# Expert rows added to the output by an accumulating scatter instead of gather, add and scatter

## The chip, the cores and the metric

The kernel runs on one core of a Trainium2 chip. The metric is the device time of one execution in microseconds; the median of the runs shown is compared. Five engines work side by side: TensorE (PE, with its weight loads PEld), VectorE (DVE), ScalarE (ACT), GpSimd (POOL) and SyncE (SP), which here only issues DMAs. They wait for each other and for DMAs through semaphores.

## What is computed

Two layers on 1024 rows (4 x 256) of 256 columns. The first is a selective scan over a context, gated by the normalised rows, and its result is added to the rows. The second, where the change lies, is a mixture of 8 experts with the top 2 chosen per row and room for 320 rows per expert:

```python
xr = x.reshape(S, d)
probs = jax.nn.softmax(xr @ Wg, axis=-1)
gate_vals, expert_idx = jax.lax.top_k(probs, K)
...
kept = pos < C                       # C = 320 slots per expert
...
dispatched = xr[dispatch_mask.reshape(-1) % S].reshape(E, C, d)
h = jax.nn.relu(jnp.einsum('ecd,edf->ecf', dispatched, w1))
expert_out = jnp.einsum('ecf,efd->ecd', h, w2)
...
out = jnp.einsum('ks,ksm->sm', combine_weights, rerouted)
...
x = x + _L0_xattn_ref(ctx_1024, _layernorm(x, axis=-1), ...)
x = x + _L0_ffn_ref(_layernorm(x, axis=-1), ...)
```

So each output row is its row after the first layer plus, for each of its two experts that had room, the gate times the expert's result.

## The kernel before

The scan layer runs first, in two halves of 512 rows; VectorE's scans set its pace. Then rows are routed: each row's two copies, 256 columns with the gate and the row's own number behind them (258 in all), are scattered by GpSimd into a table in HBM, `expert_rows`, of 8 x 320 slots (`send`, L309). This table was filled early by SyncE from one constant row, `fill` (L214), in which the gate is 0 and the row number 8192, beyond the last row. So a slot that no row took carries a number that later DMAs skip. SyncE also stores the rows after the first layer, `x1`, to `out` (L233).

Then come the 8 experts, one after the other. For each of them SyncE loads the slots' rows `xe` and the weights `w1raw` and `w2raw`, 1024 KB each. Every product is done in three matmuls, of a rounded part (`...hi`) and the rest (`...lo`) of each operand, in chunks of 320 columns. ScalarE makes the `hi` parts. VectorE makes `w1lo`, `xtlo` and `htlo`, and GpSimd makes `w2lo` in four pieces per expert (`low_w2`, L345), the last two of which only VectorE makes for expert 7. TensorE runs the first product (`xthi`, `w1hi`, 8 chunks, L864 to L866), the second (`hthi`, `w2hi`, 8 chunks, six matmuls each, the same lines), and the turning of the rows (L873) and of the results (L882). The results of expert e - 1 are turned after the second chunk of expert e's first product. For experts 0 to 6 TensorE, ScalarE and VectorE loop; GpSimd's and SyncE's streams are written out.

The results go to `out` as follows. GpSimd gathers, with three indirect DMAs per expert (128, 128 and 64 rows), the 320 output rows so far into `so_far` (`fetch`, L350; L358). It may do so only when the scatters of the expert before have landed (`res_out`). VectorE multiplies a turned result by the gate, adds `so_far` and writes `eo` (`gated_rows`, L1256; L1263), between its fourth and fifth `htlo` of the next expert. GpSimd scatters `eo` to `out` with three indirect DMAs (`send_results`, L362; L367), between the second and third piece of `w2lo` of the next expert. For the last expert all this stands at the end of the program.

A DMA on GpSimd's queue (q0) is built by GpSimd itself, which is busy for it (`DMA_INDIRECT` rows); SyncE's (q1) are not.

Of the kernel before, what the change touches and what calls it, by code (L numbers as in the profile page):

```python
# [28 lines left out]
P = 128  # L29
# [18 lines left out]
DROPPED = 8192.0  # L48
EPS = 1e-5
# [5 lines left out]
NCONST = CIOTA + NE  # L55
# [19 lines left out]
def build(nc, x, ctx_t, inproj_t, xproj_t, dtproj_t, conv_w, chan, wg, w1, w2, consts, slot_numbers, sel,  # L75
# [3 lines left out]
    with ExitStack() as ctx:  # L79
# [56 lines left out]
        def sm(name, shape, dt=F32):  # L136
# [43 lines left out]
        so_far = sb("so_far", [P, ET, DM])  # L180
# [16 lines left out]
            "h_psum hthi_done htlo_done o_psum o_done r_psum so_far_set so_far_in0 so_far_in1 so_far_in2 r_done res_out x1_out dve_step").split()}  # L197
# [5 lines left out]
        def _(sp):  # L203
            sp.dma_start(inps, inproj_t).then_inc(s["inp_in"], 16)
            for hb in range(HALVES):
# [7 lines left out]
            sp.wait_ge(s["fill_made"], 1)  # L213
            sp.dma_start(xe_dram.rearrange("(t p) r -> p t r", p=P),  # L214
                         fill[:, None, :].to_broadcast([P, SLOTS // P, ROW])).then_inc(s["xe_filled"], 16)

# [46 lines left out]
        def _(pool):  # L263
# [3 lines left out]
            nc.gpsimd.memset(fill[:, 0:DM + 1], 0.0)  # L267
            nc.gpsimd.memset(fill[:, DM + 1:ROW], DROPPED).then_inc(s["fill_made"], 1)

# [68 lines left out]
            pool.wait_ge(s["xe_filled"], 16)  # L338
# [12 lines left out]
            def fetch(e):  # L351

                pool.wait_ge(s["meta_done"], 2 * (e + 1))
                if e >= 1:

                    pool.wait_ge(s["res_out"], 16 * ET * e)
                for t in range(ET):
                    nc.gpsimd.indirect_dma_start(  # L358
                        so_far[0:EROWS[t], t, :], None, out,
                        bass.IndirectOffsetOnAxis(ap=dst[0:EROWS[t], e * ET + t, :], axis=0),  # L360
                        bounds_check=T - 1, oob_is_err=False).then_inc(s[f"so_far_in{t}"], 16)

            def send_results(e):

                for t in range(ET):
                    pool.wait_ge(s["r_done"], ET * e + t + 1)
                    nc.gpsimd.indirect_dma_start(  # L367
                        out, bass.IndirectOffsetOnAxis(ap=dst[0:EROWS[t], e * ET + t, :], axis=0),
                        eo[0:EROWS[t], t, :], None, bounds_check=T - 1, oob_is_err=False
                    ).then_inc(s["res_out"], 16)  # L370


            pool.wait_ge(s["xthi_done"], KC)
            nc.gpsimd.memset(so_far[:], 0.0).then_inc(s["so_far_set"], 1)
            pool.wait_ge(s["so_far_set"], 1)
            pool.wait_ge(s["x1_out"], 16 * HALVES)
            for e in range(NE):
                pool.wait_ge(s["w2_in"], 16 * (e + 1))

                for m in range(WP // 2 if e == NE - 1 else WP):  # L380
                    low_w2(e, m)
                    if m == WP // 2 - 1 and e >= 1:
                        send_results(e - 1)
                fetch(e)
            send_results(NE - 1)


# [584 lines left out]
        def _(dve):  # L972
# [283 lines left out]
            def gated_rows(e):  # L1256

                dve.wait_ge(s["r_psum"], e + 1)
                for t in range(ET):

                    dve.wait_ge(s[f"so_far_in{t}"], 16 * (e + 1))
                    rows = slice(0, EROWS[t])
                    nc.vector.scalar_tensor_tensor(  # L1263
                        out=eo[rows, t, :], in0=ps[rows, 6 + t // 2, (t % 2) * DM:(t % 2 + 1) * DM],
                        scalar=gates[rows, bass.ds(e * ET + t, 1), 0], in1=so_far[rows, t, :],
                        op0=ALU.mult, op1=ALU.add).then_inc(s["r_done"], 1)
# [36 lines left out]
            expert(0, True, False)  # L1303
            with dve.Fori(1, NE - 1) as e:
                expert(e, False, False)
            expert(NE - 1, False, True)
# [54 lines left out]
```

## Time and profile before

| | us |
|---|---|
| three runs | 354.39, 355.7, 356.2; median 355.7 |
| profiled execution, span | 353.9 |
| TensorE busy | 276.9 (78%) |
| VectorE busy | 266.8 (75%) |
| GpSimd busy | 234.3 (66%) |
| ScalarE busy | 170.6 (48%) |
| GpSimd: 24 gathers into `so_far` | 28.4 |
| GpSimd: 24 scatters to `out` | 23.7 |

The page of the profile has a span only, from the first to the last instruction; the time of a run is measured around it. The rows further down are of five views. The table by stage gives each engine's busy time in a stretch of the span. The chain of waits follows the work that ended last back to the start. The timeline shows single instructions of an engine, with the idle time before each in brackets and what ended it. The groups by line give counts and means, and the DMA view the queues and issues. Matmuls overlap in the pipeline: a row of TensorE shows 0.31 us, but the next one starts 0.15 us later.

### The profile page before, as it was taken

The page shows a single profiled execution, that of the slowest core. Times are in us where ns is not written, and L with a number is a line of the kernel's source. Part 1 is how long each engine was busy: PE and PEld are TensorE (multiplying, and loading weights), DVE is VectorE, ACT ScalarE, POOL GpSimd, SP SyncE. Part 2 cuts the span into 40 slices and gives each one's busy share as a digit, 9 for nine tenths or more (in the row PEclk, how much of TensorE's full clock was granted, in tenths as well). Part 3 has the DMA queues.
Part 4 walks back from the last instruction along what each step waited for, and adds up shares of the span by engine and source line. Part 5 has one row for each costly group of instructions (what it writes and reads, how often), then busy time and mean ns, then how long its engine had stood idle before and what let it go on. Part 6 is the DMA issues. An engine that isn't in the chain of part 4 may idle for free.

```text
span 353.9 us, 5109 instructions
## 1 busy us (share of the span) xinstructions
PE 276.9 (78%) x1684; PEld 242.0 (68%) x1684; DVE 266.8 (75%) x373; ACT 170.6 (48%) x308; POOL 234.3 (66%) x144
## 2 busy tenths in 40 slices
PE   7889187746456588666669698889999999999970
PEld 6334175635346377555569688889999999999970
DVE  1489999999999999999997664167566675857610
ACT  0498366654825423327741236084647474554600
POOL 0125999987799948443548248738686777768643
PEclk9969679896959986988888879999999999999995
DMA  7940000000030000000005502654645545454210
GB/s 253 303 115 3 0 0 1 2 0 0 0 119 3 0 0 2 0 1 2 1 15 210 189 23 100 217 179 172 245 161 190 184 148 183 159 216 174 89 49 33
DMA packets 13504, 33.10 MB, mean 94 GB/s; under 512 B 2602, under 2 KB 9268, under 8 KB 11216
## 3 DMA queue, kind: packets, MB, share of 16 engines
q1 hardware_dynamic: 10240, 25.92, 21.7%
q0 software_dynamic: 2816, 6.32, 5.1%
q10 hardware_dynamic: 432, 0.65, 0.7%
q8 instruction: 9, 0.15, 0.2%
q14 instruction: 7, 0.06, 0.0%
HBM read 25.50 MB, written 8.43 MB: 96 GB/s over the span
## 4 chain that ended last, share of the span: by engine, by line
PE 33%; DVE 31%; issue 15%; DMA 8%; POOL 5%; ACT 4%; SPq 1%; POOLq 0%; DVEq 0%
DVE h L1061 16%; PE ps L864 9%; PE ps L866 8%; PE ps L865 8%; DVE hc L1072 4%; POOL expert_rows L316 4%; DMA xnat<-in_x 2%; PE ps L680 2%; DMA w1raw<-in_w 2%; PE ps L873 2%; DMA expert_rows<-xrow,sloti 2%; PE ps L882 1%; DVE dbu L1180 1%; DVE delta L1026 1%; PE ps L851 1%
## 5 line engine op out<-in xcount | busy, mean ns | idle before, releaser
L293 POOL TENSOR_TENSOR dbu<-du,bsb 128x1024 f32<-128x1024 f32 x30 | 101.1, 3392 | 29.0 <-DVE h L1061 23.1
L1061 DVE TENSOR_TENSOR_SCAN h<-da,dbu 128x1024 f32<-128x1024 f32 x32 | 100.6, 3144 | 0.1
L680 PEld LDWEIGHTS ps<-cst,hc 128*128 128x128 f32 x512 | 74.7, 225 | 5.5 <-issue 2.2
L680 PE MATMUL ps<-cst,hc 128*128 128x128 f32 x512 | 74.6, 309 | 0.0
L673 PE MATMUL ps<-stack,sels 96*128 96x512 bf16 x32 | 14.4, 451 | 55.3 <-DVE hc L1072 55.3
L1252 DVE SCALAR_TENSOR_TENSOR htlo<-ps,hthi 128x320 fp32r<-128x320 f32 x64 | 30.4, 486 | 34.1 <-ACT hthi L588 34.0
L462 ACT ACTIVATE bsb<-ps 128x512 f32<-128x512 f32 x32 | 18.8, 593 | 63.1 <-PE ps L667 61.9
L348 POOL TENSOR_TENSOR w2lo<-w2raw,w2hi 128x512 fp32r<-128x512 f32 x30 | 38.2, 1300 | 12.8 <-ACT w2hi L579 12.6
L673 PEld LDWEIGHTS ps<-stack,sels 96*128 96x128 bf16 x32 | 3.2, 101 | 63.0 <-DVE hc L1072 54.1
L480 ACT ACTIVATE da<-delta,anegs 128x510 f32<-128x510 f32 x64 | 41.9, 712 | 0.0
L864 PE MATMUL ps<-xthi,w1hi 128*128 (+1 forms) x128 | 40.6, 317 | 1.0 <-DVE w1lo L1169 1.0
L864 PE MATMUL ps<-hthi,w2hi 128*128 128x320 f32 x128 | 40.4, 315 | 1.3 <-issue 1.3
L866 PE MATMUL ps<-xthi,w1lo 128*128 (+1 forms) x128 | 39.7, 310 | 0.0
L865 PE MATMUL ps<-xtlo,w1hi 128*128 (+1 forms) x128 | 39.6, 310 | 0.0
L866 PE MATMUL ps<-hthi,w2lo 128*128 128x320 f32 x128 | 39.6, 309 | 0.0
L865 PE MATMUL ps<-htlo,w2hi 128*128 128x320 f32 x128 | 39.5, 309 | 0.0
L1072 DVE TENSOR_TENSOR hc<-h,ps 128x1024 f32<-128x1024 f32 x32 | 38.1, 1191 | 0.3 <-PE ps L680 0.3
L588 ACT ACTIVATE hthi<-ps 128x320 fp32r<-128x320 f32 x64 | 27.6, 436 | 14.8 <-PE ps L866 14.8
L316 POOL DMA_INDIRECT expert_rows<-xrow,sloti x16 | 22.0, 1377 | 19.2 <-issue 10.3
L367 POOL DMA_INDIRECT out<-eo,dst x24 | 23.7, 986 | 16.5 <-DVE eo L1263 11.9
L358 POOL DMA_INDIRECT so_far<-out,dst x24 | 28.4, 1182 | 8.7 <-issue 6.0
L1169 DVE TENSOR_TENSOR w1lo<-w1raw,w1hi 128x512 fp32r<-128x512 f32 x32 | 31.9, 1055 | 2.1 <-ACT w1hi L518 2.1
(142 smaller groups left out, 483.2 us busy)
## 6 DMA issues: line engine op xcount, KB each, us to landing
w1raw<-in_w SPq DMA_DIRECT2D x8, 1024.0 KB
w2raw<-in_w SPq DMA_DIRECT2D x8, 1024.0 KB, 4.8
expert_rows<-fill SPq DMA_DIRECT2D x1, 2580.0 KB, 17.8
xe<-expert_rows SPq DMA_DIRECT2D x8, 258.0 KB, 5.7
xnat<-in_x SPq DMA_DIRECT2D x1, 1024.0 KB, 8.7
out<-x SPq DMA_DIRECT2D x2, 512.0 KB, 4.1
sels<-in_sel SPq DMA_DIRECT2D x1, 768.0 KB, 9.9
xe<-expert_rows SPq DMA_DIRECT2D x8, 64.5 KB, 5.5
```

Source lines behind the costliest of these rows:

```text
L293: nc.gpsimd.tensor_tensor(dbu[r][:], du[:, :, halves(hb)], bsb[r][:, None, :].to_broadcast([P, EC, HT]), ALU.mult).then_inc(s["dbu_done"], 1)
L316: nc.gpsimd.indirect_dma_start(xe_dram, bass.IndirectOffsetOnAxis(ap=sloti[:, j, k:k + 1], axis=0), xrow[:, j, k, :], None, bounds_check=S ...
L348: nc.gpsimd.tensor_tensor(w2lo[:, fs, :], w2raw[:, fs, :], w2hi[:, fs, :].bitcast(F32), ALU.subtract).then_inc(s["w2lo_done"], 1)
L480: nc.scalar.activation(da[g % RING][:, c, :].rearrange("p (b l) -> p b l", b=HB)[:, :, 1:L], delta[:, c, halves(hb)].rearrange("p (b l) -> ...
L680: ins = nc.tensor.matmul(y[:, t, c * P:(c + 1) * P], hc[par][:, c, t * P:(t + 1) * P], ident, start=False, stop=last, skip_group_check=True)
L864: nc.tensor.matmul(out_, hi_a, hi_b, start=start, stop=False)
L865: nc.tensor.matmul(out_, hi_a, lo_b, start=False, stop=False)
L866: return nc.tensor.matmul(out_, lo_a, hi_b, start=False, stop=stop)
L1061: nc.vector.tensor_tensor_scan(h[r][:].rearrange("p c t -> p (c t)"), da[r][:].rearrange("p c t -> p (c t)"), dbu[r][:].rearrange("p c t - ...
L1072: nc.vector.tensor_tensor(hc[r % SUMS][:], h[r][:], ps[:, bank:bank + 1, :].to_broadcast([P, EC, HT]), ALU.mult).then_inc(s["mult_done"], 1)
L1169: nc.vector.tensor_tensor(w1lo[:, :, cols], w1raw[:, :, cols], w1hi[:, :, cols].bitcast(F32), ALU.subtract).then_inc(s["w1lo_done"], 1)
L1252: nc.vector.scalar_tensor_tensor(out=htlo[:, f, :], in0=ps[:, f % 4, 0:CAP], scalar=0.0, in1=hthi[:, f, :].bitcast(F32), op0=ALU.max, op1= ...
```

## The change

The gather `fetch`, its buffer `so_far`, the memset of it and four semaphores are gone. VectorE's `gated_rows` multiplies by the gate alone, with a `tensor_scalar`, and waits before that until all scatters of the expert before have landed. The scatters to `out` (`add_results`) now add to the rows in HBM (`compute_op=ALU.add`). `out` has 320 more rows, which the host cuts off. An empty slot carries the number of one of them in place of 8192: `fill` is all zeros, and a second DMA on SyncE writes a constant column of spare row numbers into the table once the fill has landed. The fill itself now waits for the constants to be loaded. VectorE's expert loop is written out.

```diff
+SPARE = CAP
+FROWS = SLOTS // P
...
+CSPARE = CIOTA + NE
+NCONST = CSPARE + 2 * FROWS
...
             sp.wait_ge(s["fill_made"], 1)
+            sp.wait_ge(s["small_in"], 64)
             sp.dma_start(xe_dram.rearrange("(t p) r -> p t r", p=P),
                          fill[:, None, :].to_broadcast([P, SLOTS // P, ROW])).then_inc(s["xe_filled"], 16)
+
+            sp.wait_ge(s["xe_filled"], 16)
+            sp.dma_start(xe_dram.rearrange("(t p) r -> p t r", p=P)[:, :, DM:ROW],
+                         cst[:, CSPARE:CSPARE + 2 * FROWS].rearrange("p (t o) -> p t o", o=2)
+                         ).then_inc(s["xe_filled"], 16)
...
-            nc.gpsimd.memset(fill[:, 0:DM + 1], 0.0)
-            nc.gpsimd.memset(fill[:, DM + 1:ROW], DROPPED).then_inc(s["fill_made"], 1)
+            nc.gpsimd.memset(fill[:], 0.0).then_inc(s["fill_made"], 1)
...
-            pool.wait_ge(s["xe_filled"], 16)
+            pool.wait_ge(s["xe_filled"], 32)
...
-            def fetch(e):
-
-                pool.wait_ge(s["meta_done"], 2 * (e + 1))
-                if e >= 1:
-
+            def add_results(e):
+
+                if e:
                     pool.wait_ge(s["res_out"], 16 * ET * e)
-                for t in range(ET):
-                    nc.gpsimd.indirect_dma_start(
-                        so_far[0:EROWS[t], t, :], None, out,
-                        bass.IndirectOffsetOnAxis(ap=dst[0:EROWS[t], e * ET + t, :], axis=0),
-                        bounds_check=T - 1, oob_is_err=False).then_inc(s[f"so_far_in{t}"], 16)
-
-            def send_results(e):
-
                 for t in range(ET):
                     pool.wait_ge(s["r_done"], ET * e + t + 1)
                     nc.gpsimd.indirect_dma_start(
                         out, bass.IndirectOffsetOnAxis(ap=dst[0:EROWS[t], e * ET + t, :], axis=0),
-                        eo[0:EROWS[t], t, :], None, bounds_check=T - 1, oob_is_err=False
+                        eo[0:EROWS[t], t, :], None, bounds_check=T + SPARE - 1, compute_op=ALU.add
                     ).then_inc(s["res_out"], 16)
 
 
-            pool.wait_ge(s["xthi_done"], KC)
-            nc.gpsimd.memset(so_far[:], 0.0).then_inc(s["so_far_set"], 1)
-            pool.wait_ge(s["so_far_set"], 1)
             pool.wait_ge(s["x1_out"], 16 * HALVES)
...
                     if m == WP // 2 - 1 and e >= 1:
-                        send_results(e - 1)
-                fetch(e)
-            send_results(NE - 1)
+                        add_results(e - 1)
+            add_results(NE - 1)
...
                 dve.wait_ge(s["r_psum"], e + 1)
+                if e:
+                    dve.wait_ge(s["res_out"], 16 * ET * e)
                 for t in range(ET):
-
-                    dve.wait_ge(s[f"so_far_in{t}"], 16 * (e + 1))
                     rows = slice(0, EROWS[t])
-                    nc.vector.scalar_tensor_tensor(
-                        out=eo[rows, t, :], in0=ps[rows, 6 + t // 2, (t % 2) * DM:(t % 2 + 1) * DM],
-                        scalar=gates[rows, bass.ds(e * ET + t, 1), 0], in1=so_far[rows, t, :],
-                        op0=ALU.mult, op1=ALU.add).then_inc(s["r_done"], 1)
+                    nc.vector.tensor_scalar(
+                        eo[rows, t, :], ps[rows, 6 + t // 2, (t % 2) * DM:(t % 2 + 1) * DM],
+                        gates[rows, e * ET + t, :], None, ALU.mult).then_inc(s["r_done"], 1)
...
-            expert(0, True, False)
-            with dve.Fori(1, NE - 1) as e:
-                expert(e, False, False)
-            expert(NE - 1, False, True)
+            for e in range(NE):
+                expert(e, e == 0, e == NE - 1)
             gated_rows(NE - 1)
...
+    consts[:, CSPARE + 1:CSPARE + 2 * FROWS:2] = T + np.arange(SLOTS).reshape(FROWS, P).T % CAP
...
-    out = nc.dram_tensor("out", [T, DM], F32, kind="ExternalOutput").ap()
+    out = nc.dram_tensor("out", [T + SPARE, DM], F32, kind="ExternalOutput").ap()
```

On GpSimd, from the scatters of expert 5's results to the end of the program (before):

```order
L367 DMA out<-eo,dst 1024x256 [waits r_done] x3
L348 TENSOR_TENSOR w2lo<-w2raw,w2hi 128x512 [waits w2hi_done] x2
L358 DMA so_far<-out,dst 128x256 [waits res_out,meta_done]
L358 DMA so_far<-out,dst 128x256
L358 DMA so_far<-out,dst 64x256
L348 TENSOR_TENSOR w2lo<-w2raw,w2hi 128x512 [waits w2hi_done,w2_in]
L348 TENSOR_TENSOR w2lo<-w2raw,w2hi 128x512 [waits w2hi_done]
L367 DMA out<-eo,dst 1024x256 [waits r_done] x3
L358 DMA so_far<-out,dst 128x256 [waits res_out,meta_done]
L358 DMA so_far<-out,dst 128x256
L358 DMA so_far<-out,dst 64x256
L367 DMA out<-eo,dst 1024x256 [waits r_done] x3
```

The same stretch after:

```order
L364 DMA out<-eo,dst 1344x256 [waits r_done,res_out]
L364 DMA out<-eo,dst 1344x256 [waits r_done] x2
L355 TENSOR_TENSOR w2lo<-w2raw,w2hi 128x512 [waits w2hi_done] x2
L355 TENSOR_TENSOR w2lo<-w2raw,w2hi 128x512 [waits w2hi_done,w2_in]
L355 TENSOR_TENSOR w2lo<-w2raw,w2hi 128x512 [waits w2hi_done]
L364 DMA out<-eo,dst 1344x256 [waits r_done,res_out]
L364 DMA out<-eo,dst 1344x256 [waits r_done] x2
L364 DMA out<-eo,dst 1344x256 [waits r_done,res_out]
L364 DMA out<-eo,dst 1344x256 [waits r_done] x2
```

The gathers with their wait for `res_out` are gone, the wait stands at the first scatter, and the third and fourth piece of `w2lo` still stand behind the three scatters.

On VectorE, the last expert's chunks to the end (before; `htlo` is the rest of a chunk of the first product, `eo` the gated results):

```order
L1252 SCALAR_TENSOR_TENSOR htlo<-ps,hthi 128x320 [waits hthi_done] x4
L1263 SCALAR_TENSOR_TENSOR eo<-ps,gates,so_far 128x256 [waits so_far_in0,r_psum]
L1263 SCALAR_TENSOR_TENSOR eo<-ps,gates,so_far 128x256 [waits so_far_in1]
L1263 SCALAR_TENSOR_TENSOR eo<-ps,gates,so_far 64x256 [waits so_far_in2]
L1252 SCALAR_TENSOR_TENSOR htlo<-ps,hthi 128x320 [waits hthi_done] x2
```

The same rows after:

```order
L1245 SCALAR_TENSOR_TENSOR htlo<-ps,hthi 128x320 [waits hthi_done] x4
L1256 TENSOR_SCALAR eo<-ps,gates 128x256 [waits res_out,r_psum]
L1256 TENSOR_SCALAR eo<-ps,gates 128x256
L1256 TENSOR_SCALAR eo<-ps,gates 64x256
L1245 SCALAR_TENSOR_TENSOR htlo<-ps,hthi 128x320 [waits hthi_done] x2
```

Nothing moved: the three waits for gathered rows became one, for the scatters of the expert before.

## Rows read from the trace of the kernel before

**Rows 1.** Table by stage: stretch, length, busy (instructions) per engine, clock, DMA share, GB/s.
```profile
224.00:240.70 16.70, 15.10 (x100) 13.63 (x98) 8.78 (x24) 8.91 (x18) 8.66 (x8) 1.00 0.70 249
...
304.50:320.40 15.90, 15.90 (x109) 15.41 (x109) 10.35 (x22) 8.91 (x18) 11.77 (x11) 1.00 0.52 184
...
336.40:354.00 17.60, 6.85 (x47) 6.31 (x45) 1.83 (x4) 0.88 (x2) 6.87 (x7) 0.74 0.13 42
```

**Rows 2.** Chain of waits at the end: start, length, what.
```profile
336.70 2.76 DMA out<-eo,dst
...
343.01 2.39 DMA so_far<-out,dst
```

**Rows 3.** Timeline of TensorE: start, length, line, operation, tiles, [idle before <- releaser].
```profile
320.34 0.41 PE L864 MATMUL ps<-hthi,w2hi 128*128 128x320 f32 x1
...
323.96 0.31 PE L864 MATMUL ps<-hthi,w2hi 128*128 128x320 f32 x1
...
342.91 0.55 PE L882 MATMUL ps<-cst,eot 128*128 128x128 f32 x3 [0.20 <-ACT eot L602]
```

**Rows 4.** Timeline of VectorE: `eo` of expert 6, then of expert 7.
```profile
332.74 1.25 DVE L1263 SCALAR_TENSOR_TENSOR eo<-ps,gates,so_far 128x256 f32<-128x256 f32 x3
...
343.49 0.48 DVE L1263 SCALAR_TENSOR_TENSOR eo<-ps,gates,so_far 128x256 f32<-128x256 f32 x1 [6.71 <-PE ps L882]
...
345.42 0.48 DVE L1263 SCALAR_TENSOR_TENSOR eo<-ps,gates,so_far 64x256 f32<-64x256 f32 x1 [0.38 <-DMA so_far<-out,dst]
```

**Rows 5.** Timeline of GpSimd: last scatter of expert 5, then those of expert 7.
```profile
320.77 0.92 POOL L367 DMA_INDIRECT out<-eo,dst  x1 [0.30 <-issue]
...
344.81 1.04 POOL L367 DMA_INDIRECT out<-eo,dst  x1 [0.86 <-DVE eo L1263]
346.15 1.00 POOL L367 DMA_INDIRECT out<-eo,dst  x1 [0.31 <-DVE eo L1263]
347.45 0.92 POOL L367 DMA_INDIRECT out<-eo,dst  x1 [0.30 <-issue]
```

**Rows 6.** Timeline of GpSimd: `w2lo` and gathers in a steady expert, and the first gather.
```profile
321.70 2.57 POOL L348 TENSOR_TENSOR w2lo<-w2raw,w2hi 128x512 fp32r<-128x512 f32 x2
...
326.06 1.46 POOL L358 DMA_INDIRECT so_far<-out,dst  x1 [0.30 <-issue]
...
329.78 1.29 POOL L348 TENSOR_TENSOR w2lo<-w2raw,w2hi 128x512 fp32r<-128x512 f32 x1 [1.02 <-ACT w2hi L579]
...
225.32 1.06 POOL L358 DMA_INDIRECT so_far<-out,dst  x1 [0.15 <-issue]
```

**Rows 7.** Timeline of TensorE: its waits in the first expert.
```profile
225.90 1.21 PE L873 MATMUL ps<-cst,xe 128*128 128x128 f32 x6 [0.63 <-DMA xe<-expert_rows]
...
231.79 0.41 PE L864 MATMUL ps<-xthi,w1hi 128*128 x1 [0.97 <-DVE w1lo L1169]
```

**Rows 8.** Chain of waits, first expert.
```profile
223.67 6.46 DMA w1raw<-in_w
```

**Rows 9.** Timeline of SyncE: the load of expert 0's first weights.
```profile
96.91 0.34 SPq L218 DMA_DIRECT2D w1raw<-in_w  x1
```

**Rows 10.** Table by stage, as rows 1, where that load has ended.
```profile
101.50:102.50 1.00, 1.00 (x4) 0.69 (x3) 1.00 (x1) 0.11 (x1) 0.99 (x1) 0.50 0.00 0
```

**Rows 11.** DMA queues from 225 to 230.12: packets, MB, share of 16 engines.
```profile
q1 hardware_dynamic: 257, 1.62, 91.5%
q0 software_dynamic: 2, 0.01, 0.4%
```

**Rows 12.** Groups by line of VectorE: count, busy us, mean ns, idle before.
```profile
L1045 DVE TENSOR_SCALAR spr<-ps,ch 128x512 f32<-128x512 f32 x2 | 1.5, 751 | 0.2 <-ACT hc L424 0.2
```

**Rows 13.** Table by stage, as rows 1, after expert 5's scatters.
```profile
322.50:323.00 0.50, 0.50 (x6) 0.50 (x5) 0.50 (x1) 0.50 (x2) 0.50 (x2) 1.00 0.00 0
```

**Rows 14.** DMA issues: count, KB each, us to landing.
```profile
expert_rows<-fill SPq DMA_DIRECT2D x1, 2580.0 KB, 17.8
```

**Rows 15.** DMA queues from 333 to 340, as rows 11.
```profile
q0 software_dynamic: 128, 0.26, 10.5%
```

More of the change, by code:

```diff
@@ L54 @@
 CIOTA = CDST + TILES
-NCONST = CIOTA + NE
+CSPARE = CIOTA + NE
+NCONST = CSPARE + 2 * FROWS
 BC = 2 * DS
@@ L179, in build @@
         eo = sb("eo", [P, ET, DM])
-        so_far = sb("so_far", [P, ET, DM])
         ps = ctx.enter_context(nc.psum_tensor("ps", [P, 8, HT], F32))
@@ L196, in build @@
             "w1hi_done w1lo_done w2hi_done w2lo_done xet_psum xthi_done xtlo_done meta_done "
-            "h_psum hthi_done htlo_done o_psum o_done r_psum so_far_set so_far_in0 so_far_in1 so_far_in2 r_done res_out x1_out dve_step").split()}
+            "h_psum hthi_done htlo_done o_psum o_done r_psum r_done res_out x1_out dve_step").split()}
         block = ctx.enter_context(nc.Block())
@@ L1356 @@
         ins[name] = nc.dram_tensor("in_" + name, a.shape, mybir.dt.from_np(a.dtype), kind="ExternalInput").ap()
-    out = nc.dram_tensor("out", [T, DM], F32, kind="ExternalOutput").ap()
+    out = nc.dram_tensor("out", [T + SPARE, DM], F32, kind="ExternalOutput").ap()
     build(nc, out=out, **ins)
     r = run_bass_kernel_spmd(nc, [feed], core_ids=[0])
-    return r.results[0]["out"].reshape(B, L, DM)
+    return r.results[0]["out"][0:T].reshape(B, L, DM)
```

## Prediction

> **What bounds the kernel now.** I read the busy shares first, then the table by stage, then the chain of waits, and last the timelines of the three places where the edited instructions sit. No engine fills the whole span, so the shares say little by themselves. The stages say more: in a steady expert TensorE is busy for the whole stretch, 15.90 of 15.90 us at a granted clock of 1.00 (the 2.4 GHz level), while GpSimd, which issues the gathers and scatters that change, is busy for 11.77 [rows 1]. There a microsecond taken off GpSimd is worth nothing, and one added costs nothing until TensorE has to wait for something that GpSimd makes. TensorE is idle in two places of the expert stage: at the first expert (busy 15.10 of 16.70 us) and at the end (6.85 of 17.60) [rows 1]. So the change can gain in these two places alone, and it can lose in all of them.
>
> The chain of waits looks as if the end held a gain. It goes from expert 6's last scatter (336.70, landing after 2.76) to the gather of expert 7's rows (the last one issued at 343.01, landing after 2.39) and on to the third `eo` [rows 2]: some 6 us, from 339.46 to 345.40, with the gather on the chain. The timeline tells another story. TensorE finishes the last transposes at 342.91 + 0.55 = 343.46 [rows 3], and VectorE's first `eo` starts at 343.49, after 6.71 us of waiting for TensorE [rows 4]: its gathered rows were already there. It ends at 343.97; GpSimd's first scatter follows 0.84 us later, at 344.81, and from there the three scatters run at GpSimd's own pace, 344.81, 346.15, 347.45, with 0.31 and 0.30 us between them [rows 5]. The third `eo` did wait 0.38 us for gathered rows, but it ended at 345.42 + 0.48 = 345.90 [rows 4]; with the same 0.84 its scatter could have gone at 346.74, and it went at 347.45. The chain follows the wait that ended last on VectorE; the pace of the scatters hides that wait.
>
> **The change part by part.** *The 24 gathers go, with `so_far`'s memset.* In the steady experts they stand between the last `w2lo` (end 321.70 + 2.57 = 324.27) and the next expert's first (329.78), which waits 1.02 us more for ScalarE's `w2hi` [rows 6]: nothing is gained, GpSimd only waits longer for the same ScalarE. At the end they run beside TensorE's last matmuls, as just shown: without them the first `eo` still starts at 343.49 and its scatter at 344.81. Gain there: 0. The memset stands ahead of expert 0's `w2lo`; TensorE would begin expert 0's second product that much sooner, and would then wait longer at 225.90 for expert 1's rows, which it does already for 0.63 us [rows 7]. Gain: 0.
>
> *The gathers' traffic goes.* TensorE's wait at 231.79 (0.97 us, for `w1lo` [rows 7]) goes back to the load of expert 1's `w1raw`, 6.46 us from its issue at 223.67 [rows 8]. The same 1024 KB for expert 0, issued at 96.91 with nothing beside them, were moved by 101.50: no byte after that [rows 9, 10]. Expert 0's gathers are issued from 225.32 on [rows 6], in the middle of the slow load; taking them out could give back up to the 0.97 us. But between 225 and 230.12 the gathers' queue moved 2 packets, 0.01 MB, against 1.62 MB on the loads' queue [rows 11]: they waited for the load, the load did not wait for them. I take 0, and keep 0.97 as the most that could be won.
>
> *VectorE multiplies by the gate and no longer adds.* One `eo` took 0.48 us for 256 columns [rows 4]. The nearest row for the new form, a `tensor_scalar` out of PSUM, is 0.751 for 512 [rows 12], so the new one lies between half of that and all of it: -0.10 to +0.27 for the first `eo` (the others are behind the pace of the scatters). It is nearest to today's 0.48, if a fixed part is allowed for; I take 0. The expert loop on VectorE is written out instead of looped; VectorE was busy 10.35 of 15.90 us [rows 1], so this costs nothing as long as the instructions arrive.
>
> *A new wait on VectorE.* Ahead of the three `eo` it now waits until the scatters of the expert before have landed, since `eo` is what they read and no gather stands between any more. Queued behind it are the later `htlo`, on which TensorE waits. In the steady state an expert's last scatter is issued at 320.77, and the DMA engines are quiet from 322.50 on [rows 5, 13]; the next `eo` comes at 332.74 [rows 4]. That is 10 us of cover. At the end it is 343.49 against 336.70 + 2.76 = 339.46, 4.0 us [rows 2, 4]. I cost it at 0.
>
> *On SyncE the fill of the slot rows* now waits for the small loads, and a second DMA writes each slot's spare row number, 2560 pieces of 8 bytes. The fill is as many pieces of 1032 bytes and took 17.8 us [rows 14]. Twice that, one after the other, ends some 40 us into the span; SyncE's next work waits until 96.91 [rows 9], and the first scatter into these rows comes far later still. 0.
>
> *The scatter accumulates.* This is where the cost is, and no row of this kernel shows such an operation. It has two prices.
>
> First its issue on GpSimd. A plain scatter takes 1.04, 1.00 and, with half the rows, 0.92 us [rows 5]: nearly all of it is fixed, and 64 rows fewer save about 0.1. An accumulating one must name the old row, the source row and the row written, three addresses in place of two; at half again of the part that grows with the rows that is 0.1 + 0.1 + 0.05 = **0.25 us** per expert. Bounds: 0 below, since nothing is left out; above, the dearest indirect DMA of the steady experts, a gather at 1.46 [rows 6], hence 3 x 1.46 - 2.96 = 1.42. I take 0.25, nearest to how the plain rows behave.
>
> What an expert can bear follows from the same timeline. GpSimd's third `w2lo` follows the scatters; one takes 1.29, so it is done at 321.70 + 1.29 = 322.99 [rows 6]. TensorE's second product starts at 320.34 and meets that `w2lo` at its fifth chunk, 323.96 [rows 3]. The slack is **0.97 us** per expert. 0.25 fits, so the steady experts stay TensorE's: 0. At the end there is no cover: **+0.25**.
>
> Second its landing, which only the last scatter shows. A plain one lands 2.76 us after its issue begins; the gather's trip is 2.39 [rows 2], less 0.92 of issue [rows 5] 1.47. If the old row were fetched, and only then the whole of the plain scatter followed, that trip would come on top. Bounds: 0 (the same bytes are still written) and 1.47. Part of that trip is the completion, which isn't paid twice, so I take **+0.8**.
>
> A scatter also writes all 320 slots now, the empty ones to spare rows; the bytes are few: three scatters moved 0.26 MB in 10.5% of 7 us, 0.74 us of all engines [rows 15]. The Trainium skill ("Collectives: The Full Stack", section "The bandwidth ceiling: the fold count and why AG ≠ RS ≠ AR") speaks against the change here: it finds that adding in the DMA path halves the rate, not through the arithmetic but because two sources are read. No run yet shows that for this queue; by it alone the last scatter's fifth of those 0.74 us would double, +0.15 in place of 0.8, and the sum would be +0.4.
>
> Sum: 0 + 0 + 0.25 + 0.8 = **+1.05 us** on the profiled execution, from a span of 353.9 to about 355.0. The median of the three runs, 355.7, lies 1.8 above that span; the same difference gives **356.7**.
>
> **The rivals.** *A. The issue outgrows its cover.* From 0.97 us per expert on, the third `w2lo` is late for TensorE, and each of the experts 1 to 6 pays the rest, shifting all that follows. For: nothing shows that an accumulating scatter is built the way of a plain one, and GpSimd alone builds it. Against: the plain rows hardly grow with their count. At the bound of 1.42 it is 6 x 0.45 = 2.7, plus 1.42 and 0.8 at the end: +4.9, 360.6. At twice the plain price (+2.96) it is 6 x 1.99 = 11.9, plus 2.96 and 0.8: +15.7, 371.
>
> *B. The cover holds, the landing is long.* 128 rows over 16 DMA engines are 8 each; if their reads and writes don't overlap, the landing grows by several trips of 1.47. Two make +2.9 + 0.25: 358.9. Eight would make 11.8, and then the wait on VectorE binds too (4.0 us of cover at the end).
>
> *C. The gather was on the path after all,* as the chain of waits says: up to the 6 us from 339.46 to 345.40 would go, 350. Against: the first `eo` started 0.03 us after TensorE. What remains possible is the 0.97 us at 231.79, which is under the measure of "no change".
>
> **How the numbers follow.** A measurement of this kernel can tell about 0.5%, 1.8 us, from no change. The forecast with its bounds (0 to +1.7, and less when the load of `w1raw` gains) has 0.53; A near its bound (+2 to +5.3) 0.21, A far above it 0.12; B from 1.8 up 0.09; C and all other gains over 1.8 us 0.05. Faster 0.05, same 0.53, slower 0.42. The range: at the low end the forecast with 0.97 won and little paid, 354.9; at the high end A's bound, 361.0. Outside lie A far above, the longest part of B, and C. The likeliest case's own range is 354.9 to 357.5.
>
> **What would show it.** In the profile after: steady experts of 15.9 us again with TensorE full, and no wait of the `hthi,w2hi` matmuls for GpSimd's `w2lo`; the first scatter of expert 7 about 1.35 us after TensorE's last transpose ends; scatters of 1.0 to 1.2 us; the end of the span about a microsecond further from the last issue. Scatters above 1.3 us and waits of TensorE for `w2lo` make it A; several us more between the last issue and the end make it B; a first scatter sooner than 1.3 us after the last transpose makes it C. The forecast is wrong if TensorE's stretch per expert grows at all.

## The result, and the profile after

The changed kernel is slower: 362.67 us, median of 4 runs (361.75 to 363.37), against 355.54 (354.39 to 356.2, 4 runs) for the kernel before. The ratio is 1.0191 (95% interval 1.0166 to 1.0216). The profiled execution has a span of 360.2 us, 6.3 more than before. The prediction said 356.7 and at most 361.0; it was wrong.

The timeline of GpSimd in the changed kernel, one steady expert and then the end (start, length, line, operation, tiles, [idle before <- releaser]):

```profile
289.13 1.56 POOL L364 DMA_INDIRECT out<-eo,dst  x1 [1.07 <-DVE eo L1256]
290.99 1.55 POOL L364 DMA_INDIRECT out<-eo,dst  x1 [0.30 <-issue]
292.84 1.43 POOL L364 DMA_INDIRECT out<-eo,dst  x1 [0.30 <-issue]
...
351.45 1.55 POOL L364 DMA_INDIRECT out<-eo,dst  x1 [5.12 <-DVE eo L1256]
353.30 1.55 POOL L364 DMA_INDIRECT out<-eo,dst  x1 [0.30 <-issue]
355.16 1.43 POOL L364 DMA_INDIRECT out<-eo,dst  x1 [0.30 <-issue]
```

They answer to [rows 5]: 1.55, 1.55 and 1.43 us in place of 1.04, 1.00 and 0.92. Three issues cost 4.53 us, 1.57 more than before. (Two of the 24 took 1.87 and 1.93 us; the mean of all is 1.56.) That is over the 0.97 us that an expert could bear, so TensorE waits. Its waits from 224 us on (engine, line, waited for: us in total, times, longest):

```profile
PE ps L857 <- POOL w2lo L355: 6.2, 6, 1.4
PE ps L866 <- DMA xe<-expert_rows: 1.1, 1, 1.1
```

The first row did not exist before. By stretch (length, then busy time and count for PE, PEld, DVE, ACT, POOL, then clock, DMA share, GB/s), 100 us of steady experts of the kernel before and, under it, of the changed one:

```profile
240.00:340.00 100.00, 100.00 (x679) 97.26 (x680) 63.80 (x123) 54.11 (x110) 72.52 (x62) 1.00 0.47 167
```

```profile
240.00:340.00 100.00, 93.80 (x630) 89.81 (x629) 65.29 (x111) 51.04 (x105) 56.36 (x41) 1.00 0.56 152
```

GpSimd is busy for 16 us less in this stretch and delays TensorE nevertheless, because of where its work stands. The chain of waits of the changed kernel through one expert (start, length, what) goes round in a loop that TensorE is hardly part of:

```profile
287.80 1.26 DVE eo L1256 x3
...
289.13 0.36 POOL out L364
...
290.99 1.55 POOL out L364
...
292.84 1.43 POOL out L364
294.27 2.56 POOL w2lo L355 x2
296.90 5.12 DMA w2raw<-in_w
...
304.25 0.45 ACT hthi L581
...
305.13 1.26 DVE eo L1256 x3
```

Scatters, the last two `w2lo`, then the reload of the one `w2raw` buffer that these two free, then ScalarE's work on it, then the next `eo` and its scatters: 17.33 us for this turn, where an expert of TensorE's work is 15.9.

The timeline of VectorE gives the rest: the first `eo` of expert 0, of expert 6 and of expert 7.

```profile
236.06 1.25 DVE L1256 TENSOR_SCALAR eo<-ps,gates 128x256 f32<-128x256 f32 x3
...
339.53 1.25 DVE L1256 TENSOR_SCALAR eo<-ps,gates 128x256 f32<-128x256 f32 x3
...
350.12 1.26 DVE L1256 TENSOR_SCALAR eo<-ps,gates 128x256 f32<-128x256 f32 x3 [6.54 <-PE ps L875]
```

In the kernel before, expert 0's stood at

```profile
237.14 1.25 DVE L1263 SCALAR_TENSOR_TENSOR eo<-ps,gates,so_far 128x256 f32<-128x256 f32 x3
```

and the other two at 332.74 and 343.49 [rows 4]. Behind the last landing SyncE waits for the program's end; I call this the close. First the kernel before, then the changed one (queue, line, waited for: us, times, longest):

```profile
SPq L79 <- PEq L79: 4.0, 1, 4.0
```

```profile
SPq L82 <- PEq L82: 1.6, 1, 1.6
```

So the 6.3 us are made up thus (the last issues end at 348.37 and 356.59):

| stretch | before | after | difference |
|---|---|---|---|
| start to first `eo` of expert 0 | 237.14 | 236.06 | -1.08 |
| six experts | 95.60 | 103.47 | +7.87 |
| expert 6's to expert 7's first `eo` | 10.75 | 10.59 | -0.16 |
| to the end of the last issue | 4.88 | 6.47 | +1.59 |
| to its landing, and from there to the end | 5.5 | 3.6 | -1.9 |

### The profile page after: what moved, and what is told of

It is laid out like the page before. It is cut to its first block, busy times and chain, and to the rows that moved or that the text cites. A ratio compares the mean times of both kernels' runs of the same rounds, so it can differ in the third digit from the quotient of the medians.

```text
span 360.2 us, 4914 instructions
## 1 busy us (share of the span) xinstructions
PE 278.0 (77%) x1684; PEld 242.1 (67%) x1684; DVE 272.8 (76%) x373; ACT 169.6 (47%) x308; POOL 218.9 (61%) x118
## 3 DMA queue, kind: packets, MB, share of 16 engines
q0 software_dynamic: 3712, 4.74, 8.5%
## 4 chain that ended last, share of the span: by engine, by line
DVE 32%; issue 19%; PE 14%; POOL 13%; DMA 12%; ACT 6%; SPq 1%; POOLq 1%; DVEq 0%; ACTq 0%
DVE h L1054 16%; DMA w2raw<-in_w 7%; POOL out L364 6%; DVE hc L1065 5%; POOL w2lo L355 4%; PE ps L857 3%; POOL expert_rows L323 2%; PE ps L859 2%; PE ps L858 2%; DMA xnat<-in_x 2%; DVE eo L1256 2%; PE ps L673 2%; ACT hthi L581 2%; DMA xe<-expert_rows 2%; DMA expert_rows<-xrow,sloti 1%
## 5 line engine op out<-in xcount | busy, mean ns | idle before, releaser
L355 POOL TENSOR_TENSOR w2lo<-w2raw,w2hi 128x512 fp32r<-128x512 f32 x30 | 40.9, 1485 | 43.1 <-ACT w2hi L572 43.1
L364 POOL DMA_INDIRECT out<-eo,dst x24 | 37.5, 1561 | 18.4 <-DVE eo L1256 13.5
L1162 DVE TENSOR_TENSOR w1lo<-w1raw,w1hi 128x512 fp32r<-128x512 f32 x32 | 37.7, 1237 | 3.2 <-ACT w1hi L511 3.2
L581 ACT ACTIVATE hthi<-ps 128x320 fp32r<-128x320 f32 x64 | 27.7, 436 | 13.3 <-PE ps L859 13.2
L857 PEld LDWEIGHTS ps<-hthi,w2hi 128*128 128x128 f32 x128 | 24.0, 188 | 9.3 <-issue 8.8
```

The lines of the kernel that those rows point to most:

```text
L355: nc.gpsimd.tensor_tensor(w2lo[:, fs, :], w2raw[:, fs, :], w2hi[:, fs, :].bitcast(F32), ALU.subtract).then_inc(s["w2lo_done"], 1)
L364: nc.gpsimd.indirect_dma_start(out, bass.IndirectOffsetOnAxis(ap=dst[0:EROWS[t], e * ET + t, :], axis=0), eo[0:EROWS[t], t, :], None, boun ...
L581: nc.scalar.activation(hthi[:, f, :], ps[:, f % 4, 0:CAP], ACT.Relu).then_inc(s["hthi_done"], 1)
L857: nc.tensor.matmul(out_, hi_a, hi_b, start=start, stop=False)
L1162: nc.vector.tensor_tensor(w1lo[:, :, cols], w1raw[:, :, cols], w1hi[:, :, cols].bitcast(F32), ALU.subtract).then_inc(s["w1lo_done"], 1)
```

## The experiments

Where a run has one execution, times below are of that one. Seventeen runs of the kernel before lie between 354.49 and 357.58 us, so steps of some tenths are read from the trace, between `eo` and `eo`, and not from such a time.

### The scatter without the add

```diff
-                        eo[0:EROWS[t], t, :], None, bounds_check=T + SPARE - 1, compute_op=ALU.add
+                        eo[0:EROWS[t], t, :], None, bounds_check=T + SPARE - 1
```

> The changed kernel with the addition taken out of the scatter: the same 24 scatters with the same spare rows overwrite instead of adding, so the second expert's result replaces the first one's. Theory (the issue of an accumulating scatter on GpSimd outgrew its cover): the scatters fall from 1.56, 1.55, 1.43 us back to about 1.04, 1.00, 0.92; the distance from one expert's first eo to the next falls from 17.2 us to 15.9; the wait of TensorE for w2lo (6.2 us in all) goes; span about 352.5. Rival (the longer issue comes from the spare rows, every slot being written, or from the bounds check that no longer skips): the scatters stay near 1.5 us and the span near 360. Rival (VectorE's written-out loop costs the time): the scatters fall, the span stays above 358.

Measured: 354.92 us, span 352.9. First the group of the scatters in the changed kernel, then in this one (line, operation, tiles, count | busy us, mean ns of one | idle before):

```profile
L364 POOL DMA_INDIRECT out<-eo,dst x24 | 37.5, 1561 | 18.4 <-DVE eo L1256 13.5 <-issue 4.9
```

```profile
L364 POOL DMA_INDIRECT out<-eo,dst x24 | 23.1, 965 | 23.4 <-DVE eo L1256 18.5 <-issue 4.9
```

The six experts are back at 15.93 us each (238.13 to 333.73), and TensorE does not wait for `w2lo`. One argument of one call carries the whole loss; spare rows, the new DMA and the written-out loop carry none of it. Both kernels write all 320 slots, so the 0.6 us an issue (1561 against 965 ns) are the price of the add alone.

### One, then two of the three scatters add

```diff
-                        eo[0:EROWS[t], t, :], None, bounds_check=T + SPARE - 1, compute_op=ALU.add
+                        eo[0:EROWS[t], t, :], None, bounds_check=T + SPARE - 1, **(dict(compute_op=ALU.add) if t in (0,) else {})
```

> The changed kernel with only the first of each expert's three scatters adding, the other two overwriting (the sums of the rows of slots 128 to 319 are left out). By the rows of before an expert bears 0.97 us more on GpSimd. Theory: the issue grows by 0.55 us, under that, and the experts stay at 15.9 us from eo to eo; span about 352.7. Rival (any lengthening costs, since the loop through w2raw has no slack): about a third of the loss, 16.4 us per expert, span about 355.

Measured: 356.62 us, span 354.5; six experts from 238.41 to 334.66, 16.04 each, and no wait of TensorE for GpSimd. 0.56 us of extra issue cost 0.11. There is a cover, as the theory said. (The span is nearer to the rival's 355, but that is the start: expert 0's `eo` came at 238.41, where the changed kernel had it at 236.06.)

With `t in (0, 1)`:

> As the run with one, but the first two of three scatters add (the sums of slots 256 to 319 are left out). Theory: the issue grows by 1.1 us, 0.13 above the cover of 0.97: 16.0 to 16.2 us from eo to eo, span 353.5 to 354.5. Rival (any lengthening costs): two thirds of the loss, 16.8 us per expert, span about 357.5.

Measured: 360.55 us, span 358.4; 238.17 to 338.20, 16.67 each. TensorE's waits:

```profile
PE ps L857 <- POOL w2lo L355: 2.8, 6, 1.0
```

About 1.1 us of extra issue cost 0.74, and the third add (1.6 in all) brings it to 1.31. The theory's 16.0 to 16.2 was missed; the rival's 16.8 is nearer. The loss begins earlier than at 0.97 and then grows by a little more than the issue grows, which suggests that something beside the third `w2lo` waits for GpSimd.

### A second buffer for w2raw

```diff
+        w2raws = [w2raw, sb("w2odd", [P, FC, DM])]
...
-                sp.wait_ge(s["w2lo_done"], WP * e)
-                sp.dma_start(w2raw[:], w2[e]).then_inc(s["w2_in"], 16)
+                sp.wait_ge(s["w2lo_done"], WP * e - 1)
+                sp.dma_start(w2raws[e % 2][:], w2[e]).then_inc(s["w2_in"], 16)
```

(and the readers of the buffer take it by the expert's parity)

> The changed kernel with a second buffer for w2raw, so that the next expert's second weights are requested when three of the four w2lo pieces are done and not behind the last. The scatters, their place and the rest stay. Theory (two things wait on GpSimd's longer issue: TensorE for the third w2lo piece, at issue minus cover, 1.58 - 0.97 = 0.6 us an expert, and the reload of the one w2raw buffer, which closes a loop scatter, w2lo, reload, w2hi, eo, scatter, and adds the other 0.7): without the second the first eo of each expert lies 16.4 to 16.6 us after the one before instead of 17.24, ScalarE's waits for w2raw (4.3 us in the changed kernel) are gone, TensorE's for w2lo stay (3 us and more), and the whole is 358 to 359 us. Rival (the excess over 0.6 comes from the w2lo pieces that run slower beside w1lo, 3.0 for 2.57 us, or from the adds' traffic): 17.1 to 17.3 us an expert and 361.5 to 363.5 us.

Measured: 362.33 us, span 360.0; 237.79 to 339.25, 16.91 each. ScalarE's waits for `w2raw` are gone, and the expert is 0.33 us shorter than the changed kernel's 17.24. The theory wanted 16.4 to 16.6 us an expert and 358 to 359 us in all, the rival 17.1 to 17.3 and 361.5 to 363.5: the experts lie between the two, the time in the rival's range. (The span is hardly shorter than the changed kernel's, 360.0 against 360.2, since expert 0's `eo` came 1.73 us later here.) So the loop of the chain above is not the price by itself: with it opened, an expert still takes 16.91. The rows say why. TensorE's waits, then a steady stretch of exactly one expert of this kernel, and under it one of the kernel before:

```profile
PE ps L859 <- POOL w2lo L356: 4.4, 6, 0.8
```

```profile
288.52:305.43 16.91, 16.19 (x110) 15.45 (x109) 11.49 (x21) 8.84 (x19) 9.63 (x7) 1.00 0.57 163
```

```profile
284.94:300.88 15.94, 15.94 (x110) 15.46 (x109) 10.38 (x22) 8.91 (x20) 11.80 (x10) 1.00 0.54 184
```

And TensorE around its stop, ahead of the fifth chunk of the second product:

```profile
295.52 0.31 PE L861 MATMUL ps<-hthi,w2lo 128*128 128x320 f32 x1
296.55 0.41 PE L859 MATMUL ps<-hthi,w2hi 128*128 128x320 f32 x1 [0.72 <-POOL w2lo L356]
296.80 0.30 PE L860 MATMUL ps<-htlo,w2hi 128*128 128x320 f32 x1
```

TensorE waits 0.73 us an expert (4.4 / 6), against 0.6 worked out, and its busy time is 16.19 where as many matmuls took 15.94 without a stop: the stop costs 0.25 us beyond the wait. The rows show where: matmuls that follow each other start 0.15 us apart, but the last one before the stop is counted for its whole 0.31, and after the first one behind the stop the next starts only 0.25 later. That is 0.16 + 0.10. And 15.94 + 0.25 + 0.73 = 16.92. (The rival's slower `w2lo` is not there: the timeline's 3.0 us for the two begin before the last scatter's row has ended, and in the chain above they take 2.56 from its end.) So of the changed kernel's 1.31 us per expert, about 0.98 are the late third `w2lo`, and up to 0.33 the late reload. The smaller share is rough: in the changed kernel's one trace the experts vary from 17.08 to 17.56 us, and with VectorE's loop rolled again (below) they take 17.05, which would leave 0.14 for the reload.

### The scatters behind all w2lo pieces

```diff
-                    if m == WP // 2 - 1 and e >= 1:
-                        add_results(e - 1)
+                if e >= 1:
+                    add_results(e - 1)
```

> The changed kernel with one move: the three accumulating scatters of expert e-1 stand behind all pieces of w2lo of expert e on GpSimd, not between the second and the third. Theory: what cost the time is only that the third and fourth w2lo stand behind a dearer issue, and with them the next load of w2raw. The scatters stay at 1.5 us each, but nothing that TensorE waits for is behind them: 15.9 us from eo to eo, no wait for w2lo, span about 352.4, time about 354.8, 0.2% under the kernel before. Rival (the accumulating transfers, longer on the DMA engines, hold back the weight loads): from eo to eo stays above 16.5 us and the span above 356.

Measured: 354.8 us (12 runs) against 355.92 (17 runs), ratio 0.9975 (0.9956 to 0.9995). The scatters are no cheaper:

```profile
L364 POOL DMA_INDIRECT out<-eo,dst x24 | 39.3, 1637 | 13.0 <-DVE eo L1256 7.1 <-issue 5.8
```

but nothing that TensorE soon waits for stands behind them. In the timeline of GpSimd all four `w2lo` run together and the adds follow:

```profile
283.15 5.05 POOL L355 TENSOR_TENSOR w2lo<-w2raw,w2hi 128x512 fp32r<-128x512 f32 x4 [5.07 <-ACT w2hi L572]
288.36 1.56 POOL L364 DMA_INDIRECT out<-eo,dst  x1 [0.16 <-issue]
290.23 1.55 POOL L364 DMA_INDIRECT out<-eo,dst  x1 [0.30 <-issue]
```

Six experts take 238.42 to 334.03, 15.93 each, as the theory said. The same adds, the same bytes on the same queue, cost the six experts nothing: the loss was the dearer issue at its place in GpSimd's order, not the traffic of the adds. This version beats both kernels, the one before by a quarter of a per cent, which is just clear of the noise. Its trace does not show that gain: the execution traced was the slowest of the twelve (357.05 us, span 354.9).

The same move in the kernel before:

> The kernel before with an expert's plain scatters behind all the w2lo pieces of the next, gathers and all else as they were; asks how much of the late run's time is the order alone. Theory (before, TensorE waits for nothing that the order changes: the steady stage is full of TensorE work at 15.90 us): same within 0.5 us, 355.0 to 356.2 us, eo 15.9 us apart. Rival (the gathers now follow the scatters' landing later, so that the sum of scatter, landing, gather and its landing does not fit in an expert any more): eo 16.1 us apart or more and 357 us or more.

Measured: 360.23 us (4 runs), ratio 1.0127 (1.0093 to 1.0161), and 16.61 us an expert (238.10 to 337.77): the rival. VectorE's timeline has the reason, in the worst expert:

```profile
301.94 0.99 DVE L1263 SCALAR_TENSOR_TENSOR eo<-ps,gates,so_far 128x256 f32<-128x256 f32 x2
306.18 0.48 DVE L1263 SCALAR_TENSOR_TENSOR eo<-ps,gates,so_far 64x256 f32<-64x256 f32 x1 [3.25 <-DMA so_far<-out,dst]
```

The gather may only follow the landing of the scatters, and its rows came too late; TensorE then waited 2.4 us for `eo`. So the late order is open only to the kernel without the gather: that is what the change is worth.

### VectorE's loop rolled again

```diff
-            for e in range(NE):
-                expert(e, e == 0, e == NE - 1)
+            expert(0, True, False)
+            with dve.Fori(1, NE - 1) as e:
+                expert(e, False, False)
+            expert(NE - 1, False, True)
```

> The changed kernel with VectorE's expert loop rolled again, as it was before. Theory (the unrolled loop costs and gives nothing): first eo of each expert 17.1 to 17.4 us apart, 361.5 to 363.5 us. Rival (a part of the excess over issue minus cover is VectorE fetching unrolled code): 16.5 to 16.9 us apart and 357 to 360.5 us.

Measured: 362.81 us, span 360.8; 237.80 to 340.12, 17.05 each, 0.05 under the range of the theory and 0.15 over the rival's, with the time in the theory's. The written-out loop is not the cause; the run without the add had it too and took 15.93. Whether it has a part in the last 0.19 us per expert, one execution does not tell.

### The kernel before without its gathers

```diff
-                fetch(e)
+                pool.wait_ge(s["meta_done"], 2 * (e + 1))
```

(and `eo` without `so_far`, as in the changed kernel)

> The kernel before with its gathers taken out and nothing else moved: plain scatters that skip rows numbered above the output, VectorE's loop as it was, and the rows of each expert overwrite instead of being summed. What is left out: the sum over experts. Question: the kernel before ends 4.07 us after its last scatter has landed, the changed one 1.67 us. Theory (GpSimd's closing work grows with the gathers that it issued): 1.5 to 2.1 us from the last landing to GpSimd's end, time 353 to 354.5 us. Rival (it comes from the skipping of rows, or from the rolled loop): about 4.0 us, time 354.8 to 356.2 us. On the head: with no gathers beside it, w1raw of expert 1 takes 5.3 to 6.0 us from its request to the first w1hi piece, 6.48 before.

Measured: 353.61 us, span 351.7. SyncE's wait at the end:

```profile
SPq L79 <- PEq L79: 2.1, 1, 2.1
```

2.1 against 4.0, with rows still skipped and the loop still rolled, as the theory said: the long close belongs to the gathers. (Whether to gathers as such or to the number of indirect DMAs, 48 against 24 in the expert stage, was not told apart.) By the two traces this is nearly all that the gathers cost the kernel before: the spans differ by 2.2 us, the close by 1.9, and the six experts take 95.60 in both. It lies where no row of the prediction was looking. On the head `w1raw` took 5.12 us, a little under the theory's range.

### The last expert alone gathers

```diff
+            pool.wait_ge(s["res_out"], 16 * ET * (NE - 1))
+            for t in range(ET):
+                nc.gpsimd.indirect_dma_start(
+                    so_far[0:EROWS[t], t, :], None, out,
...
+            add_results(NE - 1)
```

(on top of the late order; the last expert's scatters are plain)

> The changed kernel with the adds of an expert behind all its w2lo pieces (as in the run with them late), and the last expert alone done in the old way: its rows so far are gathered once the adds of expert 6 have landed, VectorE adds them, and its three scatters are plain. The spare rows of the output are set to zero once, early. If the last expert's accumulating issues and their longer landing are what its end costs (3 x 0.55 to 0.6 on the issues, 0.5 on the landing, against the plain form), and three gathers do not bring back the long close (4.07 us in the kernel before, 1.67 after), 2.0 us come off the late run: 352.3 to 353.3 us. Rival 1 (any gather brings the long close, or the gathers land too late for VectorE, which wants them at 343 us): 354.3 to 356 us. Rival 2 (the close grows with the number of gathers, 24 before and 3 here): between, 352.8 to 353.6 us.

Measured: 355.51 us (12 runs), ratio to the kernel before 0.9997 (0.9975 to 1.0019): no gain over the late order. The close stays short, 2.2 us, so rival 2 and the first half of rival 1 fall, but the gathers land too late, the second half of rival 1. VectorE:

```profile
345.70 0.48 DVE L1270 SCALAR_TENSOR_TENSOR eo<-ps,gates,so_far 128x256 f32<-128x256 f32 x1 [8.29 <-DMA so_far<-out,dst]
```

That `eo` comes 12.34 us after expert 6's in place of 10.75. The 1.6 us lost are about the 1.5 that the cheaper issues give back.

### Expert 0's gathers made small

```diff
-                        so_far[0:EROWS[t], t, :], None, out,
+                        so_far[0:16 if e == 0 else EROWS[t], t, :], None, out,
```

> The kernel before with expert 0's three gathers cut to 16 rows each, and nothing else; what is left out: most rows that expert 0 would add to. Theory (in the first expert the load of w1raw runs beside the gathers and is slowed by them): from its request to the first w1hi piece 5.4 to 5.9 us, 6.48 before, and TensorE's wait of 0.97 for w1lo there is gone or under 0.3 us; the time is 354.3 to 355.3 us. Rival (the gathers do nothing to the load, and the changed kernel's earlier w1raw comes from something else): 6.3 to 6.6 us, a wait of 0.8 to 1.1 us, 355.0 to 356.2 us.

Measured: 354.83 us, span 353.0. The first `w1hi` of expert 1 on ScalarE, in this kernel and then in the changed one:

```profile
229.26 2.19 ACT L518 ACTIVATE w1hi<-w1raw 128x512 fp32r<-128x512 f32 x4 [1.94 <-DMA w1raw<-in_w]
```

```profile
229.10 2.19 ACT L511 ACTIVATE w1hi<-w1raw 128x512 fp32r<-128x512 f32 x4 [1.39 <-DMA w1raw<-in_w]
```

From the request of `w1raw` (223.30 here, 223.50 there) this is 5.96 and 5.60 us, against 6.48 before: just over the theory's range, and under the rival's. TensorE's wait for `w1lo` shrank to 0.58 from 0.97, less than the theory said. Over all runs: 6.48 and 6.24 in the two kernels with all of expert 0's gathers, 5.12 to 5.92 in eight without any, but 6.47 in the run with the second buffer, which has none either. So the gathers seem to slow this load, by 0.3 to 1.4 us, and something else can too.

Whether that is time is another matter, since TensorE's clock differs there between the runs. The table by stretch has, in the run without the add,

```profile
228.00:230.00 2.00, 2.00 (x10) 2.00 (x10) 0.82 (x1) 0.53 (x1) 0.00 (x0) 0.58 1.06 426
```

a granted clock of 0.58, near the 1.2 GHz level, where the kernels before and after kept 1.00 (the 2.4 GHz level). The same stretch shows 0.50 to 0.60 in six runs, all without gathers beside that load; in all six TensorE had waited 1.1 to 1.9 us for expert 1's rows (`xe`) before. But it had waited 1.35 and 1.49 us in two runs that kept 1.00, so what makes the clock fall is not shown. From the request of `w1raw` to expert 0's first `eo` it takes 13.47 and 13.20 us with all gathers, 12.08 to 12.92 with none or small ones where the clock stayed at 1.00, and 13.46 to 13.77 without gathers where it fell. Expert 0's first `eo` thus lies anywhere from 236.06 to 238.42 in the runs with no gather beside that load, and the -1.08 of the table above is one draw of that; it can't be counted as a gain.

## Why the prediction was wrong, step by step

*The issue of the accumulating scatter* is the step that failed. It was taken at +0.25 us an expert, with 1.42 as the upper bound; it is +1.57. The reasoning was that the price of a plain issue is nearly all fixed, so that a third address could only add to the part that grows with the rows. The add is a fixed price too: 0.51 us for 64 rows and for 128 about as much (1.43 for 0.92, 1.55 for 1.04 and 1.00). The bound was no bound either, since it came from a plain operation; nothing in the trace was an add. And 0.97 lay between the value taken and that bound, so the whole verdict hung on a term that no row showed. The signs that the prediction named for rival A, scatters above 1.3 us and TensorE waiting for `w2lo`, are both there.

*The cover of 0.97 us* was read correctly for the wait that it is of, TensorE for the third `w2lo`: with one add the cover nearly held (0.11 us lost), and with the reload out of the way, 1.57 - 0.97 = 0.60 showed as a wait of 0.73. But rival A's formula (each expert pays the rest) left out two things. A TensorE that stops loses 0.25 us beyond the wait. And the pieces behind the scatters free `w2raw`, whose reload was already late in the kernel before, as ScalarE's waits in its steady stage show, a row that the prediction did not use. It stands here for the kernel before (237 to 330 us) and, below, the changed one (237 to 340):

```profile
ACT w2hi L579 <- DMA w2raw<-in_w: 1.0, 5, 0.3
```

```profile
ACT w2hi L572 <- DMA w2raw<-in_w: 5.1, 6, 1.1
```

By the formula six experts would have paid 6 x 0.60 = 3.6 us; they paid 7.87. With it, rival A at the measured issue would have given some 361.7 (355.7 + 3.6 + 1.57 + 0.8), a microsecond under the measured 362.67: it was the right mechanism, with the right place, and was given a chance of 0.33.

*The landing* was taken at +0.8 us in bounds of 0 to 1.47. From the end of the last issue to its landing (348.37 to 349.59, and 356.59 to 358.31, by the last semaphore event of each) it is 1.72 us in place of 1.22, +0.5. The close after that was not in the sum at all: it shortens by 2.4 us (4.0 to 1.6), of which 1.9 also went where the gathers alone were taken out; the rest is not explained. Rival B did not occur; its 8 rows per DMA engine were those of a scatter of 128 rows, and the last one has 64.

*The gathers' removal* was costed at 0, by the row that showed VectorE's first `eo` at the end waiting for TensorE. That was right for the path that it was about: the first scatter of expert 7 follows the `eo` by 1.33 us, 1.32 before, and rival C fell. It was wrong as a price of the gathers: about 2 us of the close were theirs.

*Their traffic* was taken at 0, up to 0.97. The reasoning, that the load did not wait for the gathers because q0 moved next to nothing beside it [rows 11], does not fit the runs: the load is 0.3 to 1.4 us faster without them in all runs but one. What that is worth in time stays open, as told above.

*The multiplication, the new wait, the fill* were right at 0: an `eo` of 128 rows takes 0.476 us in both; VectorE never waits for a landing; the fill with the second DMA is done far ahead of 96.91.

*The adds' traffic* was not in the sum either, beyond the few bytes of the empty slots. For the same 4.74 MB on GpSimd's queue, the packets took (queue: packets, MB, share of 16 engines' span) in the changed kernel and, below, without the add:

```profile
q0 software_dynamic: 3712, 4.74, 8.5%
```

```profile
q0 software_dynamic: 1792, 4.74, 3.9%
```

That is 30.6 us of all engines (8.5% of 360.2) against 13.8, in twice the packets. Both sums hold the scatters of the routing, which add nothing and take 5.8 us in each (13.1 to 13.2% of the 44 us from 180 to 224); without them it is 24.8 against 8.0, a factor of 3.1. In the late order, with the same packets, the share is 7.1% of 354.9, and the factor 2.4; that run shows that nothing waited for it. The Trainium skill ("Collectives: The Full Stack", section "The bandwidth ceiling: the fold count and why AG ≠ RS ≠ AR") finds for collectives that an add in the DMA path halves the rate. The trace agrees that the add costs rate, but by more than that, a factor of 2.4 to 3.1; these are times of packets beside other transfers, not a rate measured alone.

## What to carry to other kernels

An operation that no row shows has no bound from rows of other operations: when the verdict turns on it, look at what stands behind it in its queue, and at each buffer that this work frees, and ask for the smallest added time at which something starts to wait. Work whose landing nobody waits for soon belongs behind the work that somebody waits for (with the gathers, which waited for the landing, the same move lost 1.3%); here a move of one call turned 1.9% lost into 0.25% won. And an engine's low busy share says nothing of its order: TensorE came to wait for GpSimd while GpSimd's busy time fell.

## What the runs showed of the hardware that was not expected

- An accumulating indirect scatter from GpSimd mostly keeps that engine for 1.55 us (128 rows of 256 floats) or 1.43 (64 rows), a plain one for 1.00 and 0.92; the add costs 0.5 to 0.6 us per issue, for 64 rows as for 128, and here doubled the queue's packets.
- SyncE's wait behind the last landing took 4.0 to 4.1 us in the kernels with 24 gathers, and 1.6 to 2.2 in those with three or none.
- A TensorE that stops for 0.73 us in a full stretch loses about 0.98.
- VectorE's `w1lo` got cheaper in the late order, 0.69 us a piece in place of 1.24. There it runs beside GpSimd's scatters, in the changed kernel partly beside GpSimd's `w2lo`. TensorE did not wait for it in the steady experts of either. The changed kernel's row, then that of the late order:

```profile
L1162 DVE TENSOR_TENSOR w1lo<-w1raw,w1hi 128x512 fp32r<-128x512 f32 x32 | 37.7, 1237 | 3.2 <-ACT w1hi L511 3.2
```

```profile
L1162 DVE TENSOR_TENSOR w1lo<-w1raw,w1hi 128x512 fp32r<-128x512 f32 x32 | 19.9, 685 | 1.3 <-ACT w1hi L511 1.2
```
